# Whole-row loads of the first inputs, with TensorE turning the rows and spreading the biases, in an LSTM-then-GRU kernel

## The reference

```
x = x + LSTM(x, h0=cond)          # Wx 512x2048, Wh 512x2048, b 2048
x = x + GRU(video=cond, seq=x)    # W, U, C: 512x512 for each of z, r, h; b_z, b_r, b_h

LSTM step: a = x_t @ Wx + b + h @ Wh;  i, f, o = sigmoid of three quarters of a, g = tanh of the last
           c = f * c + i * g;  h = o * tanh(c)                       (c starts at 0)
GRU step:  z = sigmoid(x_t @ W_z + g @ U_z + cond @ C_z + b_z)
           r = sigmoid(x_t @ W_r + g @ U_r + cond @ C_r + b_r)
           hh = tanh(x_t @ W + (r * g) @ U + cond @ C + b_h)
           g = (1 - z) * g + z * hh                                  (g starts at 0)
```

## Time and profile before

| | us |
|---|---|
| median of 3 runs | 1206.99 |
| lowest, highest | 1205.36, 1207.92 |
| the profiled execution | 1206.86 |
| its span in the trace | 1205.1 |
| TensorE busy in the span | 1176.5 (98%) |
| VectorE | 980.0 (81%) |
| ScalarE | 463.8 (38%) |
| GpSimd | 343.6 (29%) |

### The profile page before, as it was taken

The page is one execution under the profiler, slowest core; times in us unless marked ns, Lnnn a source line. Parts: engine busy times, 40 slices in busy tenths (PEclk is TensorE's granted clock), DMA queues, the critical chain, the costliest instruction groups (busy, mean ns, idle before and its releaser), DMA issues.

```text
span 1205.1 us, 75517 instructions
## 1 busy us (share of the span) xinstructions
PE 1176.5 (98%) x34486; PEld 859.5 (71%) x34486; DVE 980.0 (81%) x2904; ACT 463.8 (38%) x1117; POOL 343.6 (29%) x628
## 2 busy tenths in 40 slices
PE   5899999999999999999999999999999999999997
PEld 1467676666667777778777777777777777777775
DVE  2769778878878888888888888888888888888876
ACT  5565334344333333333333333333333333333332
POOL 3101233333222322322322233232232323323221
PEclk9899999999999999999999999999999999999999
DMA  9901311110011110111110011111001111101001
GB/s 313 327 10 21 143 21 22 21 21 9 17 21 21 22 22 6 20 22 21 22 22 16 10 21 22 21 22 22 11 15 22 22 21 22 21 9 18 13 13 21
DMA packets 142672, 44.17 MB, mean 37 GB/s; under 512 B 135888, under 2 KB 136144, under 8 KB 140816
## 3 DMA queue, kind: packets, MB, share of 16 engines
q1 hardware_dynamic: 140656, 38.68, 13.4%
q0 software_dynamic: 640, 0.53, 0.2%
q10 hardware_dynamic: 1056, 0.13, 0.1%
HBM read 30.93 MB, written 8.39 MB: 33 GB/s over the span
## 4 chain that ended last, share of the span: by engine, by line
PE 94%; SPq 3%; DMA 1%; DVE 1%; issue 0%; ACT 0%; DVEq 0%
PE ps_g L981 39%; PE ps_l L981 34%; PE ps_l L1044 15%; PE ps_g L990 3%; PE ps_c L1044 2%; SPq L298 2%; DMA o_area<-in_L_cond_C_dram 1%; PE ps_l L990 1%; SPq L302 1%; DVE zr L668 0%; SPq L309 0%; ACT zr L578 0%; DVE rg L901 0%; SPq L307 0%; DVE rgT L903 0%
## 5 line engine op out<-in xcount | busy, mean ns | idle before, releaser
L981 PE MATMUL ps_l<-wh,h2T 128*32 128x512 f16 x5952 | 344.4, 379 | 0.0
L981 PE MATMUL ps_g<-w,y2T 128*32 128x384 f16 x5760 | 256.1, 326 | 1.8 <-issue 1.8
L981 PEld LDWEIGHTS ps_l<-wh,h2T 128*32 128x32 f16 x5952 | 155.6, 97 | 133.5 <-issue 0.8
L981 PEld LDWEIGHTS ps_g<-w,y2T 128*32 128x32 f16 x5760 | 157.6, 97 | 91.3 <-issue 2.2
L423 POOL TENSOR_TENSOR yT<-xT,hT 128x128 f32<-128x128 f32 x128 | 61.8, 483 | 541.8 <-DVE hT L838 541.8
L981 PE MATMUL ps_g<-u,g2T 128*32 128x256 f16 x5760 | 179.1, 273 | 0.0
L981 PEld LDWEIGHTS ps_g<-u,g2T 128*32 128x32 f16 x5760 | 155.4, 97 | 15.3
L668 DVE SCALAR_TENSOR_TENSOR zr<-ps_g,sc,term 128x256 f32<-128x256 f32 x128 | 61.9, 483 | 80.0 <-PE ps_g L981 76.5
L376 POOL TENSOR_TENSOR o_area<-yT,gT 128x128 f32<-128x128 f32 x127 | 58.1, 458 | 192.3 <-DVE gT L962 191.4
L981 PE MATMUL ps_g<-u,rg2T 128*32 128x128 f16 x5760 | 102.4, 219 | 2.8 <-DVE rg2T L662 2.6
L606 ACT ACTIVATE g2T<-gT,sc 128x128 f16<-128x128 f32 x120 | 48.3, 402 | 131.7 <-DVE gT L962 131.7
(11 more groups left out here) (128 smaller groups left out, 1805.5 us busy)
## 6 DMA issues: line engine op xcount, KB each, us to landing
x_nat<-in_x_dram SPq DMA_DIRECT2D x126, 64.0 KB, 2.7
out_dram<-o_area SPq DMA_DIRECT2D x124, 64.0 KB, 2.0
wh<-in_L_cond_Wx_dram SPq DMA_DIRECT2D x4, 1024.0 KB, 10.9
stage<-in_L_cond_Wx_dram SPq DMA_DIRECT2D x4, 1024.0 KB, 9.2
w<-in_L_cond_Wh_dram SPq DMA_DIRECT2D x3, 1024.0 KB, 20.0
u<-in_L_cond_Wh_dram SPq DMA_DIRECT2D x1, 1024.0 KB, 24.8
stage<-in_L_cond_W_z_dram SPq DMA_DIRECT2D x1, 1024.0 KB, 8.7
stage<-in_L_cond_W_r_dram SPq DMA_DIRECT2D x1, 1024.0 KB, 8.0
```

The source lines that it names most:

```text
L981: mm = nc.tensor.matmul(bank[B * j:B * j + B, c0:c1].rearrange("p (n c) -> p n c", c=B), still(a, k), moving(b, k, j), start=opens and (a, ...
```

## The change

Five things, all at the start.

1. x's groups 0 and 1 are each loaded by one transfer as whole rows: partition 4b + t holds the 512 numbers of sequence b at step t. SP issues group 0, ScalarE's queue issues the condition (32 whole rows, into the memory of `yT`) and group 1. Later groups are loaded as before.
2. GpSimd makes a 128x128 unit matrix (`unit`): a fill and an `affine_select`. TensorE turns the rows of a group by four 128x128 transposes into a PSUM bank (`turn_rows`) and the condition by four into `ps_c`; VectorE copies the results to `xT` and `h0T`. Group 1 is turned between wx's first and second slab.
3. The biases are loaded as one row on one partition (`biases`, in the last slab of `stage`), first the LSTM's, then the GRU's three. TensorE spreads them by products with ones (`spread`), 4 matmuls of one row each; VectorE copies the results to `term0` and `term1`.
4. The GRU's bias transfers are issued only when the LSTM's have been spread, and U (whose last matrix covers that slab) only when both have. VectorE's copy of `term1` stands between the second low part of wx and `tick(0)`.
5. The largest of x's group 1 and the turning of group 1 leave `tick(0)` and `tick(1)`; they stand in VectorE's prologue now. The counts of the later waits on `x_in` follow.

```diff
...
         ones = sbuf("ones", [P, P])
+        unit = sbuf("unit", [P, P])
...
         yT = sbuf("yT", [P, Q, P])
+        h0_rows = yT[0:B].rearrange("b q c -> b (q c)")
...
         bias1_in = sem("bias1_in")
+        unit_made = sem("unit_made")
+        rows_ps = sem("rows_ps")
+        spread_ps = sem("spread_ps")
+        term_done = sem("term_done")
...
+        biases = stage[0:1, GG + 2, :]
...
-            for j in range(J // 2):
-                sp.dma_start(x_nat[rows(j), 0, :].rearrange("b (n p) -> b n p", p=B), natural(x, 0)[j]).then_inc(x_in[0], 16)
+
+            sp.dma_start(x_nat[:, 0, :], x[:, 0:Q, :]).then_inc(x_in[0], 16)
...
-            load(Q, 1)
...
+            sp.wait_ge(spread_ps, 2)
...
         def _(pool):
-            for j in range(J):
-                pool.dma_start(h_nat[rows(j), :].rearrange("b (k p) -> b k p", k=K), cond.rearrange("b (k j p) -> j b k p", k=K, j=J)[j]
-                               ).then_inc(h0_in, 16)
-            for j in range(J):
-                pool.dma_start(term0[rows(j), :, :].rearrange("b g (k p) -> b (g k) p", k=K),
-                               b0.rearrange("(o n j p) -> j o n p", o=1, n=GL * K, j=J)[j].to_broadcast([B, GL * K, B])
-                               ).then_inc(bias0_in, 16)
+            nc.gpsimd.memset(unit[:], 1.0).then_inc(unit_made, 1)
+            pool.wait_ge(unit_made, 1)
+            nc.gpsimd.affine_select(unit[:], unit[:], pattern=[[1, P]], compare_op=ALU.is_equal, fill=0.0, base=0,
+                                    channel_multiplier=-1).then_inc(unit_made, 1)
+            pool.dma_start(biases, b0.rearrange("(o n) -> o n", o=1)).then_inc(bias0_in, 16)
+
+            pool.wait_ge(spread_ps, 1)
             for g, b in enumerate((b_z, b_r, b_h)):
-                for j in range(J):
-                    pool.dma_start(term1[rows(j), P * g:P * g + P].rearrange("b (k p) -> b k p", k=K),
-                                   b.rearrange("(o k j p) -> j o k p", o=1, k=K, j=J)[j].to_broadcast([B, K, B])
-                                   ).then_inc(bias1_in, 16)
+                pool.dma_start(biases[:, D * g:D * g + D], b.rearrange("(o n) -> o n", o=1)).then_inc(bias1_in, 16)
...
         def _(act):
-            for j in range(J // 2, J):
-                act.dma_start(x_nat[rows(j), 0, :].rearrange("b (n p) -> b n p", p=B), natural(x, 0)[j]).then_inc(x_in[0], 16)
+            act.dma_start(h0_rows, cond).then_inc(h0_in, 16)
+            act.dma_start(x_nat[:, 1, :], x[:, Q:2 * Q, :]).then_inc(x_in[1], 16)
...
-
-            dve.wait_ge(x_in[0], 16 * J)
-            turn(0)
-            dve.wait_ge(h0_in, 16 * J)
-            nc.vector.transpose(h0T[:], h_nat[:]).then_inc(h0T_done, 1)
+            def rows_turned(r):
+
+                dve.wait_ge(rows_ps, 1 + 2 * r)
+                nc.vector.tensor_copy(xT[:, r, :].rearrange("p (t k b) -> p t k b", t=Q, k=K),
+                                      ps_g[r][:].rearrange("p (k b t) -> p t k b", k=K, t=Q)).then_inc(xT_done, 1)
+
+
+            rows_turned(0)
+            dve.wait_ge(rows_ps, 2)
+            nc.vector.tensor_copy(h0T[:], ps_c[:, 0:P]).then_inc(h0T_done, 1)
+            dve.wait_ge(x_in[1], 16)
+            largest(1)
+            rows_turned(1)
+
+            dve.wait_ge(spread_ps, 1)
+            nc.vector.tensor_copy(term0[:].rearrange("p g c -> p (g c)"), ps_bound[:]).then_inc(term_done, 1)
...
             wx_low(1)
-            dve.wait_ge(bias0_in, 16 * J)
+            dve.wait_ge(spread_ps, 2)
+            nc.vector.tensor_copy(term1[:], ps_g[0][:, 0:GG * P]).then_inc(term_done, 1)
+            dve.wait_ge(term_done, 2)
...
                     wx_low(2)
-                    dve.wait_ge(x_in[1], 16 * J)
-                    largest(1)
                 if t == T_WH:
                     common(0, 0)
-                    turn(1)
...
-                    dve.wait_ge(bias1_in, 16 * GG * J)
...
                 if q == 3 and group + 2 < NG_W:
-                    dve.wait_ge(x_in[r], 16 * J * (i + 2))
+                    dve.wait_ge(x_in[r], 16 + 16 * J * (i + 1))
...
+            def turn_rows(r):
+                for k in range(K):
+                    mm = nc.tensor.transpose(ps_g[r][:, P * k:P * k + P], x_nat[:, r, P * k:P * k + P], unit[:])
+                mm.then_inc(rows_ps, 1)
+
+            def spread(bank, columns):
+
+                for j in range(J):
+                    mm = nc.tensor.matmul(bank[rows(j), 0:columns].rearrange("p (n c) -> p n c", c=B), ones[0:1, 0:B],
+                                          biases[:, 0:J * columns].rearrange("p (n j c) -> p j n c", j=J, c=B)[:, j],
+                                          start=True, stop=True)
+                mm.then_inc(spread_ps, 1)
+
             pe.wait_ge(zeroed, 3)
+            pe.wait_ge(unit_made, 2)
+            pe.wait_ge(x_in[0], 16)
+            turn_rows(0)
+            pe.wait_ge(h0_in, 16)
+            for k in range(K):
+                mm = nc.tensor.transpose(ps_c[:, B * k:B * k + B], h0_rows[:, P * k:P * k + P], unit[0:B, 0:B])
+            mm.then_inc(rows_ps, 1)
...
+                if k == 1:
+                    pe.wait_ge(x_in[1], 16)
+                    turn_rows(1)
+                if k == 2:
+                    pe.wait_ge(bias0_in, 16)
+                    spread(ps_bound, GL * P)
...
+            pe.wait_ge(h0T_done, 1)
             pe.wait_ge(wx_squares, K)
             squares(0, K)
+            pe.wait_ge(bias1_in, 16 * GG)
+            spread(ps_g[0], GG * P)
...
+
+                    pe.wait_ge(term_done, 2)
...
```

## The result

| | before | after |
|---|---|---|
| median, us | 1206.87 (1205.36 to 1207.92, 6 runs) | 1200.07 (1199.48 to 1200.66, 6 runs) |
| profiled execution | 1206.86 | 1200.66 |
| its span | 1205.1 | 1198.9 |

The ratio is 0.9939, interval 0.9929 to 0.995: 6.8 us faster by the medians, 6.2 by the profiled executions. Forecast were 2.6 us, 1204.3, with 1200.2 as the low end. It came out on the side of the first rival (1201.9, down to 1200.2), 0.1 us beyond its fast end, which was also the end of the stated range.

A forecast was written before the change was run, and what follows sets the result against it. TensorE is full from 62.68 us on, so only an earlier start of that stretch pays. Mask 8.8, squares 24.8, gates 32.5, GRU state 56.2, start 60.0: 2.6 us off 1206.86 gives 1204.3 us, range 1200.2 to 1207.2.

The forecast's parts named there:

- the first rival: The unit matrix is ready early, 4.0 us or under 6.4; transfers bind, gain 5.0, 1201.9 us, down to 1200.2; chance 0.33.
- The mask: GpSimd's unit matrix for TensorE's turning: ready at 8.8 us, including 6.8 us for GpSimd's configuration ahead of the selection.
- step 0's gates: VectorE's addition of the first recurrent step's gates: predicted at 32.5 us, against 32.74 before.
- the closed stretch: TensorE's gapless work from the first recurrent GRU step's candidate product: start predicted at 60.0 us, against 62.68 before.
- M: Time when GpSimd's unit matrix is ready, predicted 8.8 us; the gain was written as 11.4 - M.
- The pace of landings: Weight slabs of wx, wh and C land 2.93 us apart instead of 3.29; C's last in at 45.2 us.
- the third rival: Small pieces don't cause the slow landings: 3.29 us a slab and the hole remain, gain 0.5, 1206.3 us; chance 0.12.
- The bias wait: Wait for the GRU's gate biases, issued behind the first spread: counted nothing, 0.7 us at worst kept for the range.
- The sign I had named for a wrong mechanism: TensorE waiting more than 1 us for the gate biases, or new gaps behind 60 us, would show the mechanism wrong.
- The late mask: Second rival: unit matrix later than 11.4 us, each microsecond beyond costing one, up to 1220.8 us; chance 0.10.
- From the gates to the GRU state turned: VectorE's work from step 0's gates to the first turned GRU state: 23.65 us, against 24.88 before.
- From the state turned to the closed stretch: VectorE's gate work and zr behind the turned GRU state: 2.15 + 1.66 us, from 56.2 to 60.0.

The follow-up runs named there:

- e13: Changed kernel with GpSimd's first addition also waiting for the end of VectorE's long operation, the low part of wx; 1201.72 us, ratio 0.995.
- e4: Changed kernel with only x's group 1 put back: small-piece transfers on SP behind wh, turned by VectorE; 1200.15 us, ratio 0.9943.
- e8: Changed kernel with e6's early bias rows, e7's filling products, and x's group 1 issued by SP behind wx; 1200.41 us, ratio 0.9943.
- e2: Changed kernel with the biases loaded by GpSimd's small-piece transfers as before, without spreading, bias copies or bias wait; 1202.17 us, ratio 0.9961.
- e6: Changed kernel with the GRU's bias rows in a place of their own, issued without waiting for the first spread; 1202.39 us, ratio 0.9961.
- e1: Changed kernel with a fill and four unused GpSimd multiplications ahead of the unit matrix, a late mask; 1201.79 us, ratio 0.9955.
- e5: The changed kernel again, unedited, on the chip and in the hour of e6, e7 and e8; 1201.26 us, ratio 0.9954.
- e10: e6's kernel with six products of ones ahead of TensorE's wait for gT of GRU step 1; 1202.39 us, ratio 0.9952.
- e12: e7's kernel measured again, unedited; 1199.08 us, ratio 0.9939.
- e14: e7's kernel with six products of ones ahead of TensorE's wait for gT of GRU step 1; 1199.56 us, ratio 0.9932.
- e11: Changed kernel with e6's early biases, e7's filling products and six products of ones ahead of the wait for gT; 1199.78 us, ratio 0.9941.
- e3: Changed kernel with x's groups 0 and 1 and the condition in small pieces, turned by VectorE, no mask; 1201.37 us, ratio 0.9953.
- e7: Changed kernel with unused products of ones, six ahead of the first turning and four ahead of wx's products; 1198.46 us, ratio 0.9928.
- e9: e1's kernel with fourteen products of ones ahead of TensorE's wait for gT of GRU step 1; 1202.4 us, ratio 0.9965.

## Why the prediction was wrong, step by step

**The mask: the step that failed.** "That bounds what a configured GpSimd costs before its first operation: 2.0 us at least, which show in that row." They don't. The row's 2.0 us belong to VectorE's operation beside it (e13), and the cost behind the configuration was nothing: 1.36 in place of 8.8. I had taken a duration for a price of the operation without looking at what ran beside it on the other engines in the same two microseconds; VectorE's row with its 2.31 us was there in the trace of before:

```profile
35.89 2.31 DVE L665 SCALAR_TENSOR_TENSOR wx<-wh,cols,wx 128x2048 f16<-128x2048 f32 x1
```

```profile
36.06 2.46 POOL L423 TENSOR_TENSOR yT<-xT,hT 128x128 f32<-128x128 f32 x1 [23.30 <-DVE hT L838]
```

From this false lower bound and an upper bound of 23.3, a geometric middle gave 6.8 us that nothing carried. It put step 0's gates at 32.5, and they stand at 30.45: these 2.05 us are most of the 2.5 by which the start of the closed stretch was missed. The 6 us that the Trainium skill (GPSIMD Engine Reference, Instruction dispatch) gives for the first call to a freshly loaded kernel, and which I had cited beside it, don't show either: the selection begins 0.08 us behind the end of the fill.

**What it would have been without it.** With M under 6.4 my own sum gives the first rival: 57.7' for the closed stretch. It started at 57.49. The agreement is partly luck. I had the transfers bind there, with C's product at 45.2; C was in at 42.3 (issued at 28.09, landed 14.2 us later), and VectorE's string bound. By my own terms it would have had the gates at 28.9 and the closed stretch at 56.4. It was held up by three things: the first slab landed at 7.53 (7.1 predicted), its products took 4.64 (4.1), and the gate biases made VectorE wait 0.70. The first slab came no sooner than before (7.58), although an issue less stood ahead of it; in e4 and e8, where x's group 1 is not loaded ahead of wx, it is in at 6.69 and 7.00, and in the profiles where both groups of whole rows are loaded ahead of it, between 7.45 and 8.93. TensorE's stall of 2.17 us among C's products hid behind VectorE.

**The pace of landings.** 2.93 us a slab predicted, 2.48 measured at the start. I had taken five slabs of before with no small pieces beside them for the full pace; what slowed those five was not tested. The direction and the cause (small pieces) were right, and e2 and e4 keep the two effects apart. In the third rival, 7.1 + 13 x 3.29 is 49.9 and not 49.6, and GpSimd's issues went from 20 to 4, not down by 20; neither slip changes the forecast.

**The bias wait: a second step that failed.** Counted nothing, with 0.7 kept for the range; measured 0.70 on VectorE, 1.99 on TensorE. This wait is on the path, and the half clock behind it too: without both, in e6, the gates stand 0.84 us sooner, of which 0.17 come from earlier squares. I had counted nothing because a transfer of 16 pieces should land fast, but the last of the three landed 6.25 us after its issue began. The sign I had named for a wrong mechanism, more than 1 us of TensorE waiting for the biases, did come. The late mask would not have hidden it: the biases are issued behind the first spread, which moves with the mask as TensorE does, and in e1, with a mask 4.9 us later, TensorE still waited 1.53 us.

**From the gates to the GRU state turned.** 23.65 predicted, 53.45 + 0.31 - 30.45 = 23.31 measured. It is 23.3 in the profiles of after, e1, e5 to e10 and e12 to e14, while the gates move between 28.33 and 31.91; VectorE's string sets the time of the GRU state in all of these, as the prediction had it. e2 and e11 have 23.8, because VectorE waited half a microsecond longer for step 1's gates; e3 and e4, which turn group 1 on VectorE and wait there for C (1.04 and 1.29 us), have 25.0 and 25.3. From the state turned to the closed stretch I had 3.8 and it took 3.73; where TensorE's clock fell in between (e1, e2, e8, e12, e14) it took 4.35 to 5.42.

**One to one behind it.** The stretch from there to the end is 1141.4 us in after, 1142.4 in before. In the profiles of the experiments it lies between 1139.3 and 1143.1, so the extra 1.0 us of the profiled gain is within what this part varies by among them. In before, a stall of 1.79 us in "issue" stands at 142 us; in after there is one of 0.26 at 134. Whether these are the 1.0 was not tested.

**The range.** Its low end came from the early mask's fast end, 1200.2. After came out at 1200.07, at 1201.26 in e5, and at 1201.72 with e13's harmless wait: the end was right for the rival and too near for a likeliest case. The chance of 0.33 for it was the real mistake, and it rests on the mask alone.

## What to carry to other kernels

Before a row's excess over its like is read as a price of the operation, look at what the other engines run in that very interval: an addition that takes 0.46 us alone took 2.46 because of its neighbour. When two unknown ends are a factor of ten apart, ask of each end whether its row really shows it; a middle between a misread row and a mere idle time is no estimate. Many small pieces cost twice, in the pace of the large transfers beside them and in the queue that issues them, and here, with only one of the two repaired, the other bound.

## What the runs showed of the hardware that I had not expected

TensorE's granted clock fell to half in a gap that VectorE's string makes, and how long the gap is depends on a stall elsewhere. Among profiles of nearly the same kernel, idle time ahead of the gT product and its duration were: 0 and 1.95 us (e7), 1.40 and 1.96 (e11), 1.80 and 1.96 (after), 2.23 and 3.47 (e14), 2.92 and 2.60 (e2), 3.23 and 3.64 (e12), 3.70 and 3.64 (e8), 4.70 and 3.49 (e1). The granted clock behind the gap reads 1.00 in the first three and falls to 0.50 in the others. It isn't a matter of the gap's length alone: behind the wait for the gate biases the clock fell after 1.19 us in e12, and in e7 it stayed at 1.00 after 1.65. In every profile with an "issue" stall of 2.2 to 2.7 us among C's products the gap was 1.8 or less; with one of 0.98 it was 2.92 (e2), and without any 3.2 or more, unless products filled it or TensorE itself came late because of C (e3 and e4, no gap). So in these profiles, where TensorE stood still earlier and off the path, it kept its clock on the path. What makes the "issue" stall, the profiles don't show. The same kernel ran at 1198.0 and at 1203.17 us (e12).

The mean granted clock of each run bears this out in part. It is 0.993 or 0.994 in the highest runs of e5 (1203.34), e6 (three above 1205), e12 (1203.17 and 1201.45) and e14 (1201.45), and 0.997 to 0.999 in the rest of those kernels' runs; in e2 it sinks from 0.997 or 0.998 at 1200.6 us to 0.993 above 1204. But not all high runs are of this kind: e9 has one of 1204.13 at 0.998, e6 one of 1203.05 at 0.998, and e10 three at 1202.4 to 1202.8 at 0.997 or 0.998, with the gap filled. Their cause stays open, and only one run of each kernel has a profile.

TensorE's first products ran at the slow pace after an idle start (4.64 us for the first slab, 2.78 later), although the granted clock of their stretches reads 1.00 (the row of 9 to 10 us above): at the start the pace has to be read from the durations, not from that column; ten products of ones ahead of them gave the 1.9 us back in e7, e11 and e14, and not in e12 (4.25), whose kernel is e7's, nor in e8. Why they fail there is not shown. The three measurements of this kernel and its near copy (e7, e12, e14: 0.9928, 0.9939, 0.9932) lie at or below the three of the changed kernel (0.9939, 0.9954, and 0.995 with e13's wait), on average by 0.0015 or 1.8 us. Run beside each other on one chip, e7 and e5 are apart by their intervals (at most 0.994 against at least 0.9942); all other pairs overlap. e7's kernel is the fastest version that the runs found.
